# Cross-attention in split float32: VectorE adds the two shares of tU between the two heads' row maxima, and five small tensors are allocated last

## The reference

```python
Q = (img_embed @ Wq).reshape(B, -1, H, D).transpose(0, 2, 1, 3)
K = (sent_embed @ Wk).reshape(B, -1, H, D).transpose(0, 2, 1, 3)
V = (sent_embed @ Wv).reshape(B, -1, H, D).transpose(0, 2, 1, 3)
score = jnp.einsum('bhqd,bhkd->bhqk', Q, K) / math.sqrt(D)
score = jnp.where(mask, score, -jnp.inf)
attn = jax.nn.softmax(score, axis=-1)
ctx = jnp.einsum('bhqk,bhkd->bqhd', attn, V).reshape(B, -1, H * D)
out = ctx @ Wo + img_embed
out = (out - mu) * jax.lax.rsqrt(var + EPS) * gamma + beta   # over the last axis
```

## Time and profile before

| | |
|---|---|
| median of 3 runs | 355.28 us (354.06 to 355.56) |
| the profiled execution's own time | 353.7 us |
| its span, first to last instruction | 351.9 us |
| PE busy | 324.7 us, 92% of the span |
| PEld busy | 295.0 us, 84% |
| DVE busy | 257.3 us, 73% |
| ACT busy | 219.4 us, 62% |
| POOL busy | 186.7 us, 53% |
| mean granted TensorE clock | 0.998 |

### The profile page before, as it was taken

The page is one execution under the profiler, slowest core; times in us unless marked ns, Lnnn a source line. Parts: engine busy times, 40 slices in busy tenths (PEclk is TensorE's granted clock), DMA queues, the critical chain, the costliest instruction groups (busy, mean ns, idle before and its releaser), DMA issues.

```text
span 351.9 us, 7399 instructions
## 1 busy us (share of the span) xinstructions
PE 324.7 (92%) x2264; PEld 295.0 (84%) x2264; DVE 257.3 (73%) x721; ACT 219.4 (62%) x601; POOL 186.7 (53%) x183
## 2 busy tenths in 40 slices
PE   8999999998999989998999989998999989997993
PEld 6988879998988878897988878897988878896782
DVE  0477667666996689766996689766996689764585
ACT  2555695667556766667556866677556866666350
POOL 1132386447655776447645776447645866446301
PEclk9999999999999999999999999999999999999999
DMA  8994523644246324454237324453337334430100
GB/s 271 365 399 148 168 79 119 198 133 129 79 156 224 119 84 147 145 183 134 99 132 221 122 92 139 152 191 119 98 133 224 119 100 131 151 120 0 32 30 30
DMA packets 46910, 50.26 MB, mean 143 GB/s; under 512 B 3504, under 2 KB 37040, under 8 KB 46896
## 3 DMA queue, kind: packets, MB, share of 16 engines
q1 hardware_dynamic: 46608, 49.56, 42.5%
q10 hardware_dynamic: 288, 0.52, 0.6%
HBM read 32.24 MB, written 17.83 MB: 142 GB/s over the span
## 4 chain that ended last, share of the span: by engine, by line
PE 49%; DVE 25%; issue 12%; ACT 7%; POOL 2%; DMA 2%; DVEq 1%; ACTq 1%; SPq 0%; POOLq 0%
PE score_bank L312 18%; PE tL_bank L312 10%; PE out_bank L312 7%; DVE tU L785 6%; PE tU_bank L312 6%; DVE neg_scores L737 5%; ACT probs L571 5%; DVE tU_lo L685 4%; DVE y_scaled L812 3%; DMA wq_raw<-in_wqT 2%; PE gL_bank L312 2%; DVE squares L758 1%; PE tL_bank L346 1%; PE spare_bank L346 1%; DVE gU L685 1%
## 5 line engine op out<-in xcount | busy, mean ns | idle before, releaser
L958 POOL TENSOR_TENSOR probs<-probs,inv_sum 128x512 f32<-128x512 f32 x64 | 69.7, 1092 | 106.3 <-DVE inv_sum L748 106.3
L981 POOL TENSOR_TENSOR pT_lo<-pT_raw,pT_hi 128x512 fp32r<-128x512 f32 x60 | 77.9, 1320 | 9.7 <-ACT pT_hi L528 9.7
L571 ACT ACTIVATE probs<-neg_scores,neg_max 128x256 f32<-128x256 f32 x128 | 63.9, 500 | 24.1 <-DVE neg_max L737 23.8
L737 DVE CUSTOM_DVE_ANT_0 neg_scores<-score_bank,mask_bias 128x256 f32<-128x256 f32 x128 | 49.3, 422 | 16.5 <-PE score_bank L312 12.0
L528 ACT ACTIVATE tL_hi<-tL_bank 128x512 fp32r<-128x512 f32 x31 | 18.5, 598 | 43.6 <-PE tL_bank L312 43.6
L758 DVE STREAM_TRANSPOSE squares<-probs 128x512 f32<-128x512 f32 x60 | 42.1, 702 | 1.8 <-POOL probs L958 1.5
L312 PE MATMUL score_bank<-ctxT_hi,gU 128*128 128x256 f32 x128 | 37.0, 289 | 0.7 <-POOL ctxT_lo L970 0.7
L312 PE MATMUL out_bank<-CU_hi,tU_hi 128*128 128x256 f32 x59 | 19.7, 334 | 18.8 <-DVE tU_lo L685 18.7
L312 PE MATMUL score_bank<-ctxT_hi,gL_lo 128*128 128x256 f32 x128 | 36.8, 288 | 0.0
L312 PE MATMUL score_bank<-ctxT_lo,gL_hi 128*128 128x256 f32 x128 | 36.2, 283 | 0.0
L312 PE MATMUL score_bank<-ctxT_hi,gL_hi 128*128 128x256 f32 x128 | 36.1, 282 | 0.0
(11 more groups left out here) (166 smaller groups left out, 993.0 us busy)
## 6 DMA issues: line engine op xcount, KB each, us to landing
scratch<-squares SPq DMA_DIRECT2D x30, 512.0 KB, 2.6
pT_raw<-scratch SPq DMA_DIRECT2D x120, 128.0 KB, 3.1
xT_raw<-in_xT SPq DMA_DIRECT2D x8, 256.0 KB, 3.9
ctxT_raw<-in_ctxT SPq DMA_DIRECT2D x8, 256.0 KB, 4.1
wo_raw<-in_wo SPq DMA_DIRECT2D x4, 512.0 KB, 13.7
x_res<-in_x SPq DMA_DIRECT2D x8, 256.0 KB, 3.0
out<-y_out SPq DMA_DIRECT2D x7, 256.0 KB, 2.7
wq_raw<-in_wqT SPq DMA_DIRECT2D x3, 512.0 KB, 7.4
```

Source lines behind the costliest of these rows:

```text
L571: nc.scalar.activation(probs[j % 2][:, n, :], neg_scores[:, n, :], ACT.Exp, bias=neg_max[:, n:n + 1], scale=-1.0, accum_out=row_sum[:, n:n ...
L737: nc.vector.tensor_tensor_reduce(out=neg_scores[:, n, :], in0=score_bank[hh][:, q, :], in1=mask_bias[:], scale=-SCALE, scalar=3.0e38, op0= ...
L958: nc.gpsimd.tensor_tensor(probs[j % 2][:, rows, :], probs[j % 2][:, rows, :], inv, ALU.mult) \
L981: nc.gpsimd.tensor_tensor(pT_lo[j % 2][:, k].rearrange("p hh (q i r) -> p (hh q) i r", q=QT, i=ROWS), pT_raw[j % 2][:, k].rearrange("p i n ...
```

## The change

It has two parts. On VectorE, `tU_sum` moves from behind both heads' maxima to between them, with the first head's reciprocal behind it; the second head's maxima come next, then `tU_lo`, and then the second head's reciprocal, which before stood ahead of `tU_lo`. In steps with `j = 0`, `centre` moves from between the two reciprocals to behind the first transpose of squares (still ahead of the low parts of g), and `normalise` from ahead of the transposes to the end of the step. The number of instructions that do work is the same. The other part moves `eps_col`, `power_col`, `neg_max`, `row_sum` and `inv_sum` to the end of the allocations, which shifts all tensors that stood behind them.

```diff
-        eps_col = sb("eps_col", [P, QT])
-        power_col = sb("power_col", [P, QT])
...
-        neg_max = sb("neg_max", [P, 2 * QT])
...
-        row_sum = sb("row_sum", [P, 2 * QT])
-        inv_sum = sb("inv_sum", [P, 2 * QT])
...
         rstd = sb("rstd", [P, QT])
+        eps_col = sb("eps_col", [P, QT])
+        power_col = sb("power_col", [P, QT])
+        neg_max = sb("neg_max", [P, 2 * QT])
+        row_sum = sb("row_sum", [P, 2 * QT])
+        inv_sum = sb("inv_sum", [P, 2 * QT])
...
                 if before:
                     t_lo_part_lower(t - OUT_LAG)
-                maxima(t, b)
+                maxima(t, b, heads=[0])
                 if before:
                     tU_sum(t - OUT_LAG)
                 inverse_sum(t, 0)
-                if ends is not None and j == 0:
-                    centre(ends)
+                maxima(t, b, heads=[1])
+                if before:
+                    t_lo_part_upper(t - OUT_LAG)
                 if j == 2 and not (isinstance(b, int) and b == B - 1):
                     lower_mask(b + 1)
                 inverse_sum(t, 1)
                 if j == 3:
                     finish_mask(b + 1)
-                if before:
-                    t_lo_part_upper(t - OUT_LAG)
-                if ends is not None and j == 0:
-                    normalise(ends)
                 if by_squares:
                     transpose_squares(t, j, 0)
+                if ends is not None and j == 0:
+                    centre(ends)
                 gU_lo_part(t + 1, 0)
                 gU_lo_part(t + 1, 1)
                 gL_lo_part(t + 1)
                 if by_squares:
                     transpose_squares(t, j, 1)
+                if ends is not None and j == 0:
+                    normalise(ends)
...
             t_lo_part_lower(STEPS - 5)
-            maxima(STEPS - 1, B - 1)
+            maxima(STEPS - 1, B - 1, heads=[0])
             tU_sum(STEPS - 5)
             inverse_sum(STEPS - 1, 0)
+            maxima(STEPS - 1, B - 1, heads=[1])
+            t_lo_part_upper(STEPS - 5)
             inverse_sum(STEPS - 1, 1)
-            t_lo_part_upper(STEPS - 5)
```

## The result

The changed kernel takes 330.53 us (median of 4 runs, 330.28 to 330.56) against 355.42 us; the ratio is 0.9305, 95% interval 0.9281 to 0.933. The profiled execution took 330.53 us itself, with a span of 328.7. The time lies inside the forecast range, 10.5 us above the forecast of 320; one of its two parts, the addresses, went the other way than I had said.

What follows compares the result with a forecast made beforehand. TensorE was taken as the bound, busy 324.7 of 351.9 us. Savings of 31.9 (27 steps), 1.9 (step 31) and 1.6 (outside), together 35.4, took 353.7 to 318.3; 1.6 for the median gave 320 us, range 313 to 332.

Steps and rivals of the forecast that it cites:

- the addresses: TensorE's float32r products: aligned operands give 0.109 us for 256 columns, 0.218 for 512; a step without waits 8.28, not 8.91.
- The walk through the new order: VectorE and ScalarE within a step: `tU_lo` done at 4.7 us, 1.1 us before TensorE asks, so the wait goes.
- The 24.9 us of waiting: TensorE, steps 4 to 31: time lost, almost all before `tU_lo`, 3.7 us for each batch element.
- New waits: TensorE, `j = 0` and `j = 1`: 0.3 us a batch element at the present matmul rate, 1.5 at the faster one.
- Step 31: Upper output products, without query products to cover a 2.4 us wait: `tU_lo` comes at 4.5 us, 1.9 us won.
- case C: Rival on the matmul rates: the addresses do nothing and only the order pays, 330 us; chance 0.12.
- that adds up as if each shift had its price: Matmul operand addresses: one shifted operand costs 0.005 us, two cost 0.012, so aligned 256-column products take 0.109.
- the fold in plain float32: Folding of C, both operands at 0: 0.216 us for 256 columns, by halves bounding aligned float32r at 0.108.
- the fold's rate without new waits: Low end of the main case, steps 4 to 31: 8.2 us a step, 221 in all, 10 us less.
- the 1.6 us added for the median over the profiled execution: Last term of the total: the runs' median stands 1.6 us above the profiled execution, taking 318.3 to 320.

Runs made afterwards that it cites:

- e4: The changed kernel with the layer norm's `centre` and `normalise` back in their old places; 330.82 us, ratio 0.9322 to the kernel before.
- e1: The changed kernel with the five small tensors allocated where they were, so new order with old addresses; 328.38 us, ratio 0.9244 to the kernel before.
- m2: The grid: no attention, matmuls of 256 and 512 columns for 64 pairs of start addresses, other engines idle; 256 columns took 0.113 to 0.120 us.
- e7: The changed kernel with four spacers, moving operands at 192 and weights at 128 modulo 256; 327.39 us, ratio 0.9223 to the kernel before.
- e6: The changed kernel with five spacers, 256-column products' moving operands at 128 and weights at 192 modulo 256; 326.6 us, ratio 0.9198 to the kernel before.
- m3: No attention: address pairs with moving operand 64 bytes short of or past weights, each behind three forerunners; short pair 0.113 or 0.118 us, past pair 0.118.
- e3: The changed kernel with five spacers, all moving operands at 0 and weights at 64 modulo 128; 327.0 us, ratio 0.921 to the kernel before.
- e9: e6 with the 192-byte spacer ahead of `gU` in place of `neg_scores`; 327.38 us, ratio 0.9226 to the kernel before.

## Why the prediction was right, and where it was wrong

**Where TensorE waits and why: right.** The walk through the new order gave the sum at 2.3 us, `tU_hi` at 3.2, head 1's maxima at 3.3, `tU_lo` done at 4.7, held by GpSimd; the trace has 2.24, 3.15, 3.40 and 4.72, with `tU_lo` at 0.62 us instead of 0.41. The 24.9 us of waiting that I had found between steps 4 and 31 are gone but for 0.1 us (243.3 against 27 x 9.006).

**New waits: too large.** I set 1.5 us for a batch element; there are none. The walk let VectorE be late in `j = 0` and `j = 1`, at a rate of TensorE that did not come about. At the rate there was it said 0.3, and e4 shows that the place of `centre` and `normalise` doesn't matter. Step 31 was set at 1.9 us won with `tU_lo` at 4.5; it came at 4.83, and the wait went from 2.4 to 0.9 us. The order alone was forecast as case C with 330 us and measured 328.4.

**The addresses: wrong, also in sign.** The step that failed is "that adds up as if each shift had its price, so I take a value near the low end". I read each operand's distance from a multiple of 128 as a cost. What counts in the rows is how the two starts lie to each other: query products had them 64 apart before, and the change made them equal. Predicted was 0.63 us a step won. Measured is 0.08 lost (9.006 against 8.927 in e1: query products +0.12, context products -0.05 and the rest nearly even), 2.15 us in the run instead of some 17 won. Of the 0.0066 us that a query product lost, the grid's table explains 0.002 (0.118 at a difference of 64, 0.120 at 0); the rest is the quick rhythm, which they had before and whose condition isn't known. No float32r product in the trace of before had both operands at 0, and the fold in plain float32 was no stand-in: 0.216 us is what it took for 256 columns, and the 0.108 that I made of it by halves is in no row. No run came near 0.109; the lowest float32r distance was 0.113. The change's addresses were an extrapolation to a place with no row. The rows did allow the other reading: both at 64 gave 0.1195, and 0 with 64 gave 0.113 either way round.

**The total.** 330.5 lies in the range only because the range took in case C, "the addresses do nothing", with 330 us and a chance of 0.12. That C is so near is luck: two errors of 2 us, the order's gain too small and the addresses' loss not foreseen, cancel. Two smaller points of the sums: the fold's rate without new waits would be 12 us less (233.6 - 221.4), not 10, and the 1.6 us added for the median over the profiled execution had no counterpart in the changed kernel, whose profiled execution took the median's 330.53. Of the pages of the Trainium skill that I set beside this, "SBUF — State Buffer", section "Who interferes with whom", has TensorE's two read ports independent, and that PE never waits on anyone. No run here shows TensorE held by another engine's access. But that the ports are independent leaves no reason for rates that go with the distance between the two operands while all other engines are idle; whether the ports are the cause is not shown. The formula of the Trainium skill's "TensorE: Matmul & The Clock Gate", section "Back-to-back issue gap" (0.109 us for 256 columns), which the page gives for a single matmul by itself, was reached by no float32r pair: the lowest was 0.113.

**Still open** is why the query products run at 0.113 before the change and in e1 (weights at 128, moving operand at 192 modulo 256), while the same pair is at 0.118 in the grid, behind all three forerunners and in e7's loop; why step 4 of e6 was quick and step 5 was not (in m3 512 columns with equal addresses, as e6's context products have them, left the pair at 0.118, but the kernel's turn was not tested apart); why the grid's quick cells stood behind a difference of 128, when a forerunner 128 apart in the other direction left the pair at 0.118 in m3; and what starts and ends the quick rhythm. A layout that keeps e1's pairs for the query products and gives them to the output products too was not tried.

## What to carry to other kernels

Where one engine waits for a result that crosses engines several times, look at what stands in the queues ahead of each hop and needs nothing from it: here a handful of instructions in another order were worth 7.6%. Put a VectorE instruction with two SBUF inputs where GpSimd isn't about to start: it took 1.26 us instead of 0.41 here. Price an address or a layout only from rows with the same relation between the operands; "both aligned" is not one. Change it apart from the rest, since a loss of 0.6% hides behind a gain of 7.6%.

## What the runs showed of the hardware

The distance between float32r matmuls back to back, at the 2.4 GHz level, goes with the start addresses of moving operand and weights against each other. For starts at multiples of 64 bytes the difference modulo 256 gives 0.118 to 0.120 us for 256 columns and 0.227 to 0.233 for 512, with equal addresses slowest for the first and fastest for the second (m2, m3, and the loops of e3 and e6 to e9). There is a second rhythm, 0.113 us, for some pairs at a difference of 64 or 192; whether a pair takes it isn't given by its addresses alone (m3, and steps 4 and 5 of e6). Both are there with all other engines idle, so no other engine is needed for them; the cause inside is not known.

VectorE's `tU_lo`, with both inputs in SBUF, took 0.41 us, but 1.26 when GpSimd's normalisation had begun 0.07 us ahead of it and 0.62 when it had begun 0.71 ahead. In all three such places it ended 0.29 us behind GpSimd's end. The row maxima, with one input in PSUM, kept their 0.42 us.
